# A gather-and-product kernel: from gathers tile by tile to gathers field by field over four tiles

## The chip, the cores and the metric

One core of a Trainium2 chip runs the kernel. The metric is the device time of one execution in microseconds (us); lower is better. Before the change the median of three runs is 652.37 us (652.29 to 653.44).

## The reference

A batch of 2048 samples, 26 index fields each, looks up 26 embedding rows of 32 float32 values; all pairs of rows of a sample are multiplied and summed; two weighted sums over rows and pairs go through a small network.

```python
embed = tables[jnp.arange(FIELD_NUM)[None, :], sparse_inputs]   # (2048, 26, 32)
p = jnp.einsum('bfe,bge->bfg', embed, embed)                    # (2048, 26, 26)
l_z = jnp.einsum('bfe,feh->bh', embed, w_z)                     # h = 256
l_p = jnp.einsum('bfg,fgh->bh', p, w_p)
l_1 = jax.nn.relu(jnp.concatenate([l_z + l_p + l_b, dense_inputs], axis=-1))
h = jax.nn.relu(l_1 @ W1 + b1)                                  # 128
return jax.nn.sigmoid(h @ Wf + bf)
```

Since p is symmetric, each pair is formed once and the two weights of a pair (`w_low`, `w_high`) are added on the chip.

## The kernel before

The samples are split in 16 tiles of 128 (one sample to a partition); four tiles make a round, because 4 x 128 columns fill one PSUM bank. All engines run their own program in order and meet at semaphores.

GpSimd (POOL, line 228) issues one indirect DMA for each tile and field, 416 in all, tile by tile and in a tile field by field. Each brings 128 rows of 32 values into `rows[:, t, 32 f : 32 (f+1)]`. The fields of a tile are two groups (0 to 15, and 16 to 25), each with one semaphore of `landed`. Before tiles 5 and 10 (`REST_BEFORE`) POOL waits until all that it has issued has landed.

ScalarE copies each landed group into PSUM (`copy_fields`, line 317). VectorE multiplies (`multiply`, line 259): for a chunk of fields g it forms the products with all fields up to the chunk's end, with one operand from the PSUM copy and the other from `rows`, and `add_up` (line 266) sums each product row of 32 into `pairs`. The chunks hold 4, 4, 4, 4, 3, 3, 2 and 2 fields, so a tile forms 383 pairs where 351 are different. The chunks make six stages; VectorE's order is multiply(stage s), then add_up(stage s-1).

TensorE turns the rows of a tile (`turn`, line 423, seven transposes by the identity into `ps_turn`), ScalarE moves them to `field_rows` (`lay_rows`, lines 174 and 175), and the same is done with `pairs` (`turn_pairs`, line 440, and `lay_pair_rows`, line 179). Once in a round TensorE sums over the fields (`sum_lz`, line 454, 14 matmuls) and over the pairs (`sum_lp`, line 465, 6 matmuls) into `ps_h0`; ScalarE applies the bias and relu (`make_hidden0`, line 340), TensorE makes `sum_h1` (lines 474 and 478), ScalarE `make_hidden1` (line 345), TensorE `sum_logit` (line 483), ScalarE the sigmoid (`make_scores`, line 351). SP stores all scores in one DMA.

ScalarE's order around these is written out by hand: the rows of tiles 4 to 7 are moved only at tiles 9 to 12, those of tiles 8 to 15 only after all 16 groups of copies. VectorE moves the second group of the last four tiles, and their pairs, after all its sums (`LATE`). So TensorE, in order, does the sums of rounds 2 and 3 after the last gather.

## Time and profile before

| what | us |
|---|---|
| median of three runs | 652.37 |
| the profiled execution | 652.55 |
| its span, first to last instruction | 650.8 |
| POOL busy in the span | 416.0 |
| VectorE busy | 436.1 |
| TensorE matmuls busy | 133.4 |
| ScalarE busy | 49.7 |

The profile is of one execution. "Busy" is the time in which an engine runs an instruction; "issue" in front of a gather is time that POOL spends between two gathers without waiting for anything that the profile shows. A line of a timeline has the start, the duration, the engine, the line of the kernel and the operation, and in brackets the idle time before it and what ended it. A float32 matmul has two records, so 14 matmuls stand as x28.

### The profile page before, as it was taken

What the parts mean: (1) busy time and instruction counts of PE and PEld (TensorE: products, weight loads), DVE (VectorE), ACT (ScalarE), POOL (GpSimd) and SP (SyncE); (2) the same over time, 40 slices, a digit from 0 to 9 for tenths busy, and PEclk for the clock granted to TensorE, in tenths of its full rate; (3) what the DMA queues carried; (4) which work ended last, traced back from release to release, by engine and by line L of the source; (5) the groups of instructions that cost most, each with busy time, mean ns of one, the idle gap of its engine ahead of it and who ended that gap; (6) DMA issues with size and microseconds to landing.
All of it is one profiled execution on the core that took longest, in us unless ns stands there. A gap on an engine that the chain in (4) does not pass through costs nothing.

```text
span 650.8 us, 1738 instructions
## 1 busy us (share of the span) xinstructions
PE 133.4 (21%) x356; PEld 62.2 (10%) x356; DVE 436.1 (67%) x249; ACT 49.7 (8%) x102; POOL 416.0 (64%) x423
## 2 busy tenths in 40 slices
PE   0000000063000000310302010100800000348996
PEld 0000000021000000100001010100300000124442
DVE  3378787878767878776958676776958767660010
ACT  0000101010000000001001020101000000013111
POOL 6777777777677777777776777777777777300000
PEclk9999999997555555565656555555955555578999
DMA  6212121212121212121111212111111111000000
GB/s 138 13 14 13 13 14 13 13 13 13 11 13 14 13 13 13 12 12 12 12 12 11 12 12 13 12 12 12 11 12 12 12 12 12 6 0 1 0 1 1
DMA packets 18200, 9.06 MB, mean 14 GB/s; under 512 B 9536, under 2 KB 18189, under 8 KB 18189
## 3 DMA queue, kind: packets, MB, share of 16 engines
q0 software_dynamic: 13312, 6.84, 15.6%
q1 hardware_dynamic: 4878, 2.11, 1.3%
q14 instruction: 7, 0.06, 0.0%
q8 instruction: 3, 0.05, 0.0%
HBM read 8.91 MB, written 0.01 MB: 14 GB/s over the span
## 4 chain that ended last, share of the span: by engine, by line
POOL 49%; issue 36%; PE 8%; another core or an unknown queue 3%; ACT 2%; DMA 1%; DVE 0%; ACTq 0%; POOLq 0%
POOL rows L228 49%; PE ps_h L454 4%; PE ps_h L465 2%; PE ps_turn L423 1%; PE ps_h L483 1%; PE ps_h L478 1%; ACT hidden L340 1%; ACT field_rows L175 1%; ACT ps_copy L317 1%; DMA rows<-in_L_rec_tables,which 1%; PE ps_pair L440 0%; PE ps_h L474 0%; DMA raw<-in_r_sparse_inputs 0%; ACT pair_rows L179 0%
## 5 line engine op out<-in xcount | busy, mean ns | idle before, releaser
L228 POOL DMA_INDIRECT rows<-in_L_rec_tables,which x416 | 415.2, 998 | 143.0 <-issue 137.8
L259 DVE TENSOR_TENSOR prod<-ps_copy,rows 128x1536 f32<-128x1536 f32 (+6 forms) x128 | 219.4, 1745 | 139.0 <-issue 110.8
L266 DVE TENSOR_REDUCE pairs<-prod 128x96 f32<-128x3072 f32 (+2 forms) x96 | 216.6, 2270 | 0.0
L423 PE MATMUL ps_turn<-ident,rows 128*128 128x128 f32 (+1 forms) x112 | 23.4, 360 | 221.2 <-DMA rows<-in_L_rec_tables,which 119.6
L465 PE MATMUL ps_h<-pair_rows,w_pair 128*128 128x512 f32 x48 | 25.4, 685 | 210.6 <-issue 209.4
L454 PE MATMUL ps_h<-field_rows,wz 128*128 128x512 f32 (+1 forms) x112 | 53.3, 632 | 35.6 <-issue 34.5
L317 ACT COPY ps_copy<-rows 128x512 f32<-128x512 f32 (+1 forms) x32 | 16.3, 509 | 528.8 <-DMA rows<-in_L_rec_tables,which 528.8
L423 PEld LDWEIGHTS ps_turn<-ident,rows 128*128 128x128 f32 (+1 forms) x112 | 16.6, 179 | 230.7 <-issue 209.6
L465 PEld LDWEIGHTS ps_h<-pair_rows,w_pair 128*128 128x128 f32 x48 | 10.3, 223 | 223.5 <-issue 221.8
L454 PEld LDWEIGHTS ps_h<-field_rows,wz 128*128 128x128 f32 (+1 forms) x112 | 22.0, 203 | 64.8 <-issue 64.8
L174 DVE COPY field_rows<-ps_turn 64x128 f32<-64x128 f32 x4 | 1.1, 283 | 37.7 <-PE ps_turn L423 37.7
L175 ACT COPY field_rows<-ps_turn 128x512 f32<-128x512 f32 (+1 forms) x28 | 13.7, 490 | 10.3 <-remote 9.2
L474 PE MATMUL ps_h<-dense_T,w_dense 13*128 13x512 f32 x8 | 5.6, 781 | 34.5 <-issue 30.3
L440 PE MATMUL ps_pair<-ident,pairs 128*128 128x128 f32 x48 | 11.2, 357 | 4.1 <-issue 4.1
L179 DVE COPY pair_rows<-ps_pair 128x384 f32<-128x384 f32 x4 | 2.2, 549 | 13.5 <-PE ps_pair L440 13.5
L478 PE MATMUL ps_h<-hidden,w 128*128 128x512 f32 x16 | 11.2, 839 | 0.0
L440 PEld LDWEIGHTS ps_pair<-ident,pairs 128*128 128x128 f32 x48 | 7.2, 182 | 12.4 <-issue 11.9
L340 ACT ACTIVATE hidden<-ps_h,lb_col 128x512 f32<-128x512 f32 x8 | 5.1, 683 | 34.4 <-PE ps_h L465 25.1
L179 ACT COPY pair_rows<-ps_pair 128x384 f32<-128x384 f32 x12 | 5.8, 484 | 13.1 <-PE ps_pair L440 12.8
L483 PE MATMUL ps_h<-hidden,wf 128*1 128x512 f32 x8 | 5.8, 813 | 0.8 <-ACT hidden L345 0.8
L278 DVE TENSOR_SCALAR dense_T<-ps_turn 13x512 f32<-13x512 f32 x4 | 2.7, 684 | 3.4 <-PE ps_turn L402 3.4
L474 PEld LDWEIGHTS ps_h<-dense_T,w_dense 13*128 13x128 f32 x8 | 1.4, 214 | 36.1 <-issue 30.5
(23 smaller groups left out, 24.9 us busy)
## 6 DMA issues: line engine op xcount, KB each, us to landing
rows<-in_L_rec_tables,which POOLq DMA_INDIRECT x416
wz<-in_L_rec_w_z SPq DMA_DIRECT2D x1, 768.0 KB
w_pair<-in_w_low SPq DMA_DIRECT2D x1, 384.0 KB
w_back<-in_w_high SPq DMA_DIRECT2D x1, 384.0 KB
raw<-in_r_sparse_inputs SPq DMA_DIRECT2D x1, 182.0 KB, 2.4
w<-in_L_rec_W SPq DMA_DIRECT2D x1, 128.0 KB
dense_in<-in_r_dense_inputs SPq DMA_DIRECT2D x1, 104.0 KB, 3.5
wz<-in_L_rec_w_z SPq DMA_DIRECT2D x1, 64.0 KB
```

The costliest lines, as they stand in the source:

```text
L175: return copy(field_rows[:, first:whole, k, :], ps_turn[:, g, 0:(whole - first) * P].rearrange("p (j b) -> p j b", b=P))
L228: nc.gpsimd.indirect_dma_start(rows[:, t, E * f:E * (f + 1)], None, table_rows, bass.IndirectOffsetOnAxis(ap=which[:, t, f:f + 1], axis=0) ...
L259: ins = nc.vector.tensor_tensor(made.rearrange("p (g f) e -> p g f e", f=f1), own.broadcast_to([P, f1 - f0, f1, E]), others.broadcast_to([ ...
L266: nc.vector.tensor_reduce(pairs[:, t, first:end], prod[:, (NS * t + s) % PRODS, 0:end - first, :], AX.X, ALU.add).then_inc(summed, 1)
L317: nc.scalar.copy(ps_copy[:, g, 0:E * (end - first)], rows[:, t, E * first:E * end])\
L340: ins = nc.scalar.activation(hidden0[:, h, :], ps_h0[:, h, :], ACT.Relu, bias=lb_col[:, h:h + 1])
L423: ins = nc.tensor.transpose(ps_turn[0:n, g, (j - first) * P:(j - first + 1) * P], rows[:, t, j * P:j * P + n], ident[:, :])
L440: ins = nc.tensor.transpose(ps_pair[:, c * P:(c + 1) * P], pairs[:, t, c * P:(c + 1) * P], ident[:, :])
L454: ins = nc.tensor.matmul(ps_h0[:, h, :], wz[0:n, j, h * P:(h + 1) * P], field_rows[0:n, j, :, :].rearrange("p t b -> p (t b)"), start=(j = ...
L465: ins = nc.tensor.matmul(ps_h0[:, h, :], w_pair[:, c, h * P:(h + 1) * P], pair_rows[:, c, :, :].rearrange("p t b -> p (t b)"), start=False ...
L478: ins = nc.tensor.matmul(ps_h1[:, :], w1[:, h, :], hidden0[:, h, :], start=False, stop=(h == HALVES - 1))
L483: nc.tensor.matmul(logit, wf[:, :], hidden1[:, :], start=True, stop=True).then_inc(logit_made, 1)
```

## The change

The order of the work becomes a round of four tiles, field by field. POOL gathers field f for the four tiles of the round, then field f+1. `rows` holds two rounds; from the third round on POOL waits until VectorE and TensorE have read the round before the last. Fields are grouped in units (four units of 4 fields, then 10 of one field), each with its own semaphore, and ScalarE copies a unit of all four tiles into one of four PSUM banks. `multiply` has one instruction for each field g over four tiles, with fields 0 to g, so that 351 pairs are formed; there are 18 stages a round, the last 12 of one field each. The waits for landed data before two of the tiles (`REST_BEFORE`) are gone.

The rows of fields 0 to 23 are turned by VectorE in blocks of 32 x 32 (`turn_rows`, 6 instructions a round, each over 128 partitions and 512 columns, into `rows_T`), and ScalarE puts the blocks in their places in `field_rows` (`lay_rows`, 32 copies a round of 32 partitions each: 16 of 512 columns and 16 of 256). The last two fields and the three blocks of pairs are turned by TensorE (4 transposes each) and evicted by ScalarE. TensorE's sums of a round are spread through it, and `sum_h1` begins with the dense part before it waits for `hidden0`.

```diff
-CHUNKS = [(0, 4), (4, 8), (8, 12), (12, 16), (16, 19), (19, 22), (22, 24), (24, 26)]
-STAGES = [(0, 3), (3, 4), (4, 5), (5, 6), (6, 7), (7, 8)]
+UNITS = [(0, 4), (4, 8), (8, 12), (12, 16)] + [(f, f + 1) for f in range(16, 26)]
+STAGES = [(0, 4), (4, 8), (8, 10), (10, 12), (12, 13), (13, 14)] + [(f, f + 1) for f in range(14, 26)]
...
-        rows = sb("rows", [P, TILES, NF * E])
+        rows = sb("rows", [P, 2, K, NF, E])
+        rows_T = sb("rows_T", [P, MOVED, K, PER, Q])
...
+            for r in range(ROUNDS):
...
+                if r >= 2:
+                    pool.wait_ge(multiplied, NS * (r - 1))
+                    pool.wait_ge(rows_turned, MOVED * (r - 1))
+                    pool.wait_ge(turned, TURNS * (r - 2) + ROW_TURN + 1)
                 for f in range(NF):
-                    nc.gpsimd.indirect_dma_start(
-                        rows[:, t, E * f:E * (f + 1)], None, table_rows,
-                        bass.IndirectOffsetOnAxis(ap=which[:, t, f:f + 1], axis=0),
-                    ).then_inc(landed[t][group_of(f)], DMA)
+                    for k in range(K):
+                        t = K * r + k
+                        nc.gpsimd.indirect_dma_start(
+                            rows[:, r % 2, k, f, :], None, table_rows,
+                            bass.IndirectOffsetOnAxis(ap=which[:, t, f:f + 1], axis=0),
+                        ).then_inc(landed[r][unit_of(f)], DMA)
...
+            def multiply(r, s):
+                n = NS * r + s
+                first, end = STAGES[s]
+                dve.wait_ge(copied, NU * r + unit_of(end - 1) + 1)
+                if n >= PRODS:
+                    dve.wait_ge(summed, n - PRODS + 1)
+                for g in range(first, end):
+                    u = unit_of(g)
+                    own = ps_copy[:, (NU * r + u) % COPIES, :, g - UNITS[u][0], :].rearrange("p k (o e) -> p k o e", o=1)
+                    at = pairs_before(g) - pairs_before(first)
+                    ins = nc.vector.tensor_tensor(products(n, s)[:, :, at:at + g + 1, :],
+                                                  own.broadcast_to([P, K, g + 1, E]),
+                                                  rows[:, r % 2, :, 0:g + 1, :], ALU.mult)
                 ins.then_inc(multiplied, 1)
...
+            def turn_rows(r, j):
+                n = chunk_fields(j)
+                for u in range(unit_of(PER * j), unit_of(PER * j + n - 1) + 1):
+                    first, end = UNITS[u]
+                    dve.wait_ge(landed[r][u], DMA * K * (end - first))
+                if r:
+                    dve.wait_ge(rows_laid, NM * (r - 1) + move_of(j) + 1)
+                nc.vector.transpose(rows_T[:, j, :, 0:n, :].rearrange("p k f b -> p k (f b)"),
+                                    rows[:, r % 2, :, PER * j:PER * j + n, :].rearrange("p k f e -> p k (f e)"))\
+                    .then_inc(rows_turned, 1)
...
+            for r in range(ROUNDS):
                 for s in range(NS + 1):
                     if s < NS:
+                        for j in range(MOVED):
+                            if s == stage_of(UNITS[unit_of(PER * j + chunk_fields(j) - 1)][0]):
+                                turn_rows(r, j)
+                        multiply(r, s)
                     if s:
+                        add_up(r, s - 1)
-            for t in range(LATE, TILES):
...
+            def lay_rows(r, m, q):
+                first, end = MOVES[m]
+                if q == 0:
+                    act.wait_ge(rows_turned, MOVED * r + end)
+                    if r:
+                        act.wait_ge(lz_summed, CH * (r - 1) + end)
+                for u in range(PER):
+                    n = sum(u < chunk_fields(j) for j in range(first, end))
+                    if n:
+                        ins = nc.scalar.copy(field_rows[Q * u:Q * (u + 1), first:first + n, :, Q * q:Q * (q + 1)],
+                                             rows_T[Q * q:Q * (q + 1), first:first + n, :, u, :])
...
+                for u, (first, end) in enumerate(UNITS):
+                    copy_fields(r, u)
+                    if r and first == 0:
+                        evict(r - 1, ROW_TURN)
+                        evict(r - 1, PAIR_TURN[-1])
+                    if r and first == 8:
+                        make_hidden0(r - 1)
+                    if 15 <= end - 1 < 19:
+                        lay_rows(r, 0, end - 16)
+                    if r and first == 17:
+                        make_hidden1(r - 1)
+                    if first == 19:
+                        evict(r, PAIR_TURN[0])
+                    if r and first == 20:
+                        make_scores(r - 1)
+                    if first == 23:
+                        lay_rows(r, 1, 0)
+                        lay_rows(r, 1, 1)
+                    if first == 24:
+                        lay_rows(r, 1, 2)
+                        lay_rows(r, 1, 3)
+                evict(r, PAIR_TURN[1])
...
+                turn_pairs(r, 0)
+                for j in range(*MOVES[0]):
+                    sum_lz(r, j)
+                sum_lp(r, 0)
+                turn_pairs(r, 1)
+                for j in range(*MOVES[1]):
+                    sum_lz(r, j)
+                turn_rows(r)
+                sum_lp(r, 1)
+                turn_pairs(r, BLOCKS - 1)
+                sum_lz(r, CH - 1)
+                sum_lp(r, BLOCKS - 1)
+                sum_h1(r)
+                sum_logit(r)
```

## Rows read from the trace of the kernel before

**Rows 1.** The page's chain of waits, shares of the span by engine.

```profile
POOL 49%; issue 36%; PE 8%; another core or an unknown queue 3%; ACT 2%; DMA 1%; DVE 0%; ACTq 0%; POOLq 0%
```

**Rows 2.** Busy us and count of instructions by engine, three stretches, PEclk after them.

```profile
3.60:258.10 254.50, 25.67 (x72) 13.63 (x72) 192.51 (x110) 13.32 (x30) 190.51 (x201) 0.80 0.22 20
258.10:560.00 301.90, 37.74 (x88) 17.21 (x88) 220.59 (x116) 17.55 (x37) 224.73 (x215) 0.55 0.17 12
560.00:651.00 91.00, 70.00 (x196) 31.35 (x196) 22.15 (x21) 17.54 (x34) 0.00 (x0) 0.88 0.00 1
```

**Rows 3.** Timeline: single gathers, and one VectorE operation beside the second.

```profile
3.64 1.10 POOL L228 DMA_INDIRECT rows<-in_L_rec_tables,which  x1 [2.05 <-DVE which L245]
...
14.89 0.96 DVE L283 TENSOR_TENSOR w_pair<-w_pair,w_back 128x768 f32<-128x768 f32 x1 [3.44 <-issue]
15.11 1.55 POOL L228 DMA_INDIRECT rows<-in_L_rec_tables,which  x1 [0.30 <-issue]
...
169.52 0.94 POOL L228 DMA_INDIRECT rows<-in_L_rec_tables,which  x1 [3.04 <-issue]
...
258.15 1.93 POOL L228 DMA_INDIRECT rows<-in_L_rec_tables,which  x1 [0.31 <-issue]
...
344.44 0.94 POOL L228 DMA_INDIRECT rows<-in_L_rec_tables,which  x1 [3.06 <-DMA rows<-in_L_rec_tables,which]
...
523.70 0.95 POOL L228 DMA_INDIRECT rows<-in_L_rec_tables,which  x1 [0.30 <-issue]
...
558.84 0.94 POOL L228 DMA_INDIRECT rows<-in_L_rec_tables,which  x1 [0.30 <-issue]
```

**Rows 4.** Groups by line and shape: busy us, mean ns of one.

```profile
L259 DVE TENSOR_TENSOR prod<-ps_copy,rows 128x512 f32<-128x512 f32 x16 | 11.1, 691 | 71.2 <-issue 71.2
L259 DVE TENSOR_TENSOR prod<-ps_copy,rows 128x2048 f32<-128x2048 f32 x16 | 36.5, 2279 | 0.0
L266 DVE TENSOR_REDUCE pairs<-prod 128x96 f32<-128x3072 f32 x16 | 53.5, 3341 | 0.0
L317 ACT COPY ps_copy<-rows 128x512 f32<-128x512 f32 x16 | 9.4, 589 | 324.8 <-DMA rows<-in_L_rec_tables,which 324.8
L317 ACT COPY ps_copy<-rows 128x320 f32<-128x320 f32 x16 | 6.9, 429 | 204.1 <-DMA rows<-in_L_rec_tables,which 204.1
```

**Rows 5.** Timeline of VectorE inside one tile.

```profile
108.56 2.35 DVE L259 TENSOR_TENSOR prod<-ps_copy,rows 128x2112 f32<-128x2112 f32 x1
110.83 2.04 DVE L266 TENSOR_REDUCE pairs<-prod 128x57 f32<-128x1824 f32 x1
```

**Rows 6.** Timeline after the last gather, all engines.

```profile
562.20 0.43 ACT L317 COPY ps_copy<-rows 128x320 f32<-128x320 f32 x1 [13.78 <-DMA rows<-in_L_rec_tables,which]
562.66 2.06 DVE L259 TENSOR_TENSOR prod<-ps_copy,rows 128x1824 f32<-128x1824 f32 x1 [5.27 <-ACT ps_copy L317]
563.09 7.68 PE L465 MATMUL ps_h<-pair_rows,w_pair 128*128 128x512 f32 x12 [93.74 <-issue]
...
576.77 3.53 DVE L266 TENSOR_REDUCE pairs<-prod 128x48 f32<-128x1536 f32 x2
...
583.50 1.12 PE L423 MATMUL ps_turn<-ident,rows 128*128 128x128 f32 x4 [5.13 <-ACT field_rows L175]
...
593.91 12.45 PE L454 MATMUL ps_h<-field_rows,wz 128*128 128x512 f32 x28 [0.55 <-ACT field_rows L175]
...
636.14 5.42 PE L465 MATMUL ps_h<-pair_rows,w_pair 128*128 128x512 f32 x12 [0.65 <-DVE pair_rows L179]
641.65 1.26 ACT L340 ACTIVATE hidden<-ps_h,lb_col 128x512 f32<-128x512 f32 x2 [19.54 <-PE ps_h L465]
...
646.04 0.69 ACT L345 ACTIVATE hidden<-ps_h,b_col 128x512 f32<-128x512 f32 x1 [3.13 <-PE ps_h L478]
646.78 1.02 PE L483 MATMUL ps_h<-hidden,wf 128*1 128x512 f32 x2 [0.78 <-ACT hidden L345]
647.84 1.10 ACT L351 ACTIVATE scores<-ps_h,bf_one 1x512 f32<-1x512 f32 x1 [1.11 <-PE ps_h L483]
```

More of the change, by code:

```diff
@@ new lines, in add_up @@
+            def add_up(r, s):
+                n = NS * r + s
+                first, end = (pairs_before(g) for g in STAGES[s])
+                dve.wait_ge(multiplied, n + 1)
+                if r and s == 0:
+                    dve.wait_ge(turned, TURNS * r)
+                nc.vector.tensor_reduce(pairs[:, :, first:end], products(n, s), AX.X, ALU.add).then_inc(summed, 1)
+            def turn_rows(r, j):
[8 more added lines that the diff above has]
+                    .then_inc(rows_turned, 1)
@@ L308, in _ @@
+                        multiply(r, s)
+                    if s:
+                        add_up(r, s - 1)
         @block.scalar
         def _(act):
-            def copy_fields(t):
-                for g in range(NG):
-                    first, end = group_fields(g)
-                    if t:
-                        act.wait_ge(multiplied, NS * (t - 1) + (FIRST_BANK if g == 0 else NS))
-                    act.wait_ge(landed[t][g], DMA * (end - first))
-                    nc.scalar.copy(ps_copy[:, g, 0:E * (end - first)], rows[:, t, E * first:E * end])\
-                        .then_inc(copied, 1)
@@ new lines, in sum_lz @@
+            def sum_lz(r, j):
+                if r == 0 and j == 0:
+                    pe.wait_ge(wz_in, DMA * 2)
+                if r and j == 0:
+                    pe.wait_ge(hidden0_made, HALVES * r)
+                if j < MOVED:
+                    pe.wait_ge(rows_laid, NM * r + move_of(j) + 1)
+                else:
+                    pe.wait_ge(evicted, TURNS * r + ROW_TURN + 1)
+                n = chunk_rows(j)
+                for h in range(HALVES):
+                    ins = nc.tensor.matmul(ps_h0[:, h, :], wz[0:n, j, h * P:(h + 1) * P],
+                                           field_rows[0:n, j, :, :].rearrange("p t b -> p (t b)"),
+                                           start=(j == 0), stop=False)
```

346 lines of the change are left out of this document (122 added, 224 removed).

## The prediction

> **What bounds the kernel now.** I read the chain of waits first. By engine, POOL's gathers hold 49% of it, "issue" 36% and TensorE 8% [rows 1]: the issue of gathers is the kernel for most of its length. Next, busy time by stretch [rows 2]. In the first two stretches, up to 560 us, POOL issues all its gathers (201 and 215) while VectorE is busy 192.5 of 254.5 and 220.6 of 301.9 us; in the third, 91 us, POOL does nothing, VectorE works 22 us and TensorE 70. So there are two parts, a part set by POOL and an end in which TensorE works off what ScalarE's and VectorE's orders put off. VectorE, though busy longer than POOL in total, waits on the gathers inside each tile.
>
> Single gathers give POOL's pace [rows 3]. The first starts at 3.64, the one after the first stretch at 258.15, the last at 558.84 us. The two waits for landed data show as idle 3.04 and 3.06 us instead of 0.30, so they cost 2.74 and 2.76 us. Without them the first 201 steps take 254.51 - 2.74 = 251.8 us, 1.25 us each; the next 214 take 300.69 - 2.76 = 297.9 us, 1.39 us each. From 258 us on, many gathers are stretched (the one at 258.15 is busy 1.93 us against 0.94). The trace doesn't name the cause, and it decides most of my range.
>
> The end [rows 6]: the last gather's data reach ScalarE at 562.20 (3.36 us after its start), VectorE's last sum ends at 576.77 + 3.53 = 580.3, and then two rounds' matmuls follow: 12.45 us for one `sum_lz`, 5.4 for one `sum_lp`, each twice, with transposes, copies and the network between. The span ends at 650.8, 92 us after the last gather began.
>
> **The change part by part.** The sum goes by the profiled execution, 652.55 us, which is 1.75 more than its span and 0.2 above the median.
>
> *Gathers.* Still 416, of the same form. The first index operations cover four tiles instead of two; by the 52- to 364-column cost they add a few tenths, so I start at 4.05. Both waits go: -5.5 us. What replaces them, the release of `rows` at rounds 2 and 3, asks for the round before the last, of which VectorE will be through some 20 us after its last gather, with 100 of the next round's 104 gathers still to go: nothing. With the stretched gathers as in the trace the last one starts at 4.05 + 251.8 + 297.9 = 553.8. If none is stretched it is 4.05 + 251.8 + 214 x 1.25 = 523.4; that is the lower bound. If all steps after the 201st are as stretched as the worst run of rows shows, see the rivals. I take the trace's value, since the instruction, its count and VectorE's load beside it stay nearly the same, and the trace shows no owner that the change removes.
>
> *VectorE.* A product instruction costs (2279 - 691) / 1536 = 1.034 ns a column, with 0.16 us on top [rows 4]; the reduce of 3072 columns fits the same line. The next starts 0.08 us before the former's end (2.27 us after one of 2.35 [rows 5]), so a step costs 1.034 ns a column + 0.08. A round has 351 pairs x 4 tiles x 32 = 44,928 columns to multiply and as many to add, 92.9 us, 44 instructions' 0.08, 3.5, and six transposes. The trace has no VectorE transpose. The nearest row is the 512-column product, 0.61 us net of overlap; I take 0.6, and as ends half (0.3) and twice (1.2) of it. Round: 100.0 us, against 109 now (436.1 / 4) and against 104 x 1.25 = 130 of gathers. VectorE stays the faster one, on average.
>
> The Trainium skill (VectorE: DVE Perf Modes, "The three transpose paths") gives 311 ns for one 128x128 bf16 block transpose; four of these would be 1.24 us by an estimate from that page, and adds 1.3 us to the end below. No row here shows it.
>
> But inside a round work grows with the field. After field g lands VectorE does the product of g and the sum of g-1, (2g + 1) x 0.1324 + 0.16 us: 5.3 at g = 19, 6.65 at 24, and 0.6 more at 19 and 23 for a transpose, against one field each 4 x 1.39 = 5.57 us. The backlog is 0.35 us when field 20 lands, 1.2 at 23, 3.7 at 25. After field 25: product 3.5, sum of 24 3.4, sum of 25 3.5. So VectorE ends 3.7 + 10.4 = 14.1 us after field 25 is in PSUM (17.5 us if the gathers step at 1.25, backlog 7.1). A round's surplus is absorbed by the next, whose first unit needs 16 gathers.
>
> *ScalarE.* Field 25's copy has 128 columns: 0.43 - 192 x 0.83 ns = 0.27 us (slope from the 512 and 320 column copies [rows 4]). It adds 32 partial copies a round, 16 x 0.59 + 16 x 0.375 = 15.4 us, and is idle nearly always; hidden. The risk is its order: eight copies (3.0 us) stand before the copy of field 24 and wait for the transpose of fields 20 to 23, which is behind VectorE's backlog. That puts field 24's copy about 1.2 + 0.6 + 3.0 + 0.3 = 5.1 us after field 23 was ready, while VectorE reaches it after 1.2 + 7.0: no wait.
>
> *TensorE.* 14 + 6 + 5 matmuls a round and few transposes, spread. In the last round `sum_lz` of fields 16 to 23 and the second block of pairs start when field 22's sum is done, about 15 us before VectorE's end, and need 1.1 + 4 x 1.8 + 1.1 + 2 x 1.8 = 13 us even at half clock (the granted clock of the second stretch is 0.55, that is mostly the 1.2 GHz level [rows 2]). They just fit.
>
> *After VectorE's last sum* [rows 6]: four transposes 1.12 and a hop 0.15; `sum_lz` of the last fields, 2 matmuls, under which the eviction (0.6) hides; `sum_lp` of the last block, 2 matmuls. A record is 12.45 / 28 = 0.44 us at full clock and 0.89 at half; the row at 563.09, first after an idle stretch, took 7.68 instead of 5.42, so five records at half. I take five of these eight at half: 5.8. Then relu 1.3, the last half of `sum_h1` 1.0, relu 0.74, logit 1.07, sigmoid 1.15 and the store to the span's end (650.8 - 648.94) 1.86. Sum 14.2 (11.4 all at full clock, 17.5 all at half).
>
> **Sum.** 553.8 + 3.36 + 0.30 (landing and copy) + 14.1 + 14.2 = 585.8 span, + 1.75 = 587.5 for a profiled execution, 587.3 as a median: **587 us**, 65 less than now. Of the 65, the end gives 60 (92 to 32), the waits 5.5.
>
> **The rivals.**
>
> *A. No stretched gathers.* What stretches them could be bound to tiles 7 and later, to their addresses in `rows` (up to 256 us none was stretched, with VectorE as busy), and `rows` shrinks to two rounds. Last gather 523.4, + 3.66 + 17.5 + 14.2 + 1.75 - 0.2 = 560 us. Against it: the trace may as well count time or gathers.
>
> *B. More stretching.* For: the gather at 15.11 was busy 1.55 us, 0.61 more than 0.94, beside a 0.96 us VectorE addition of two SBUF operands [rows 3]; transposes might do the same, 24 x 0.61 = 14.6: 602 us. And if all 415 steps take the 1.39 of the second stretch: 4.05 + 577 + 3.66 + 14.1 + 14.2 + 1.55 = 615 us. Against: products and sums run beside the first 201 gathers without a trace.
> The Trainium skill (SBUF — State Buffer, "SBUF: two separate sides") says that VectorE and GpSimd share a port pair as an exclusive lock, and that a VectorE operation in a two-port mode keeps GpSimd from writing DMA descriptors. By that rule the transposes, which read and write SBUF, would hold gathers up; it speaks for B, and the gather at 15.11 agrees with it; whether a transpose runs in such a mode no row shows.
>
> *C. VectorE becomes the bound, slower than before.* Place: `multiply`, whose instruction now spans four tiles, with a PSUM operand repeated over fields and stepped over tiles. Time is then 28 (first unit) + 4 x VectorE's round + 16, less where it is hidden. It reaches 652 when a round costs 152 us instead of 100, or 1.6 ns a column; at half rate, 2.07 ns, a round is 193 and the time some 816 us. Against: all product shapes of before, which already repeat and step, keep 1.03 ns. A transpose of 9 us would do it too.
>
> *D. The change doesn't shorten the end*, since TensorE's order leaves a round's sums behind VectorE's last. At half clock all 20 matmuls, 35 us, after it give 587 + 28 = 615, still faster. Against: the waits let 16 of them go before.
>
> **Chances.** Forecast (576 to 595) 0.45; A 0.25; B and D (595 to 640) 0.23; C 0.04; costs not seen here that cancel much or all of the gain, 0.03, a third of it on each side and a third at no change. Range: 557 to 613, from A with 3 us less in the end, to B's 615. Own range of the forecast 576 to 595, from the end's 11.4 to 17.5, the transposes' 0.3 to 1.2 and a third of the stretching more or less. A measurement of this kernel tells 0.2% (1.3 us) from nothing: faster 0.94, same 0.01, slower 0.05.
>
> **What would show it.** Right: POOL's last gather starts near 554, no idle of 3 us inside its queue, VectorE ends 18 us and the span 32 us after that gather. The gather steps in the profile after tell forecast (1.39 in the second half) from A (1.25 all through) and B (1.39 from the start). VectorE's transposes near 0.6 us, products on the line of 1.034 ns. Wrong: POOL idle at the start of rounds 2 or 3; VectorE idle under `copied` at fields 20 to 25; products over 1.1 ns a column; more than 18 us between VectorE's last sum and the end.

## The result and the profile after

The changed kernel took 694.21 us (median of 4 runs, 690.35 to 694.82) against 652.43 for the kernel before: ratio 1.0621, 95% interval 1.0598 to 1.0644, so 6% slower. The forecast was 587. The profiled execution took 694.79 us, its span 692.9.

What follows needs one fact ahead. Kernels of one series run on one chip beside the kernel before, and the kernel before took 652 to 654 us in six series, the first comparison among them, but 609.6 and 608.6 in two others. In those two the variants of the changed kernel are faster as well, and the changed kernel itself, measured in the second of them, wins: 573.63 against 608.6 us, 0.9439 (0.9402 to 0.9477). I call the first kind held and the second free, after what the traces show, and compare ratios only inside a series. The kernel before has no trace of the free kind.

The chain and three groups of the page, kernel after (the chain answers [rows 1]):

```profile
another core or an unknown queue 39%; issue 28%; POOL 13%; DVE 8%; ACT 7%; PE 2%; DMA 1%; DVEq 1%; ACTq 0%
...
L219 POOL DMA_INDIRECT rows<-in_L_rec_tables,which x416 | 426.0, 1024 | 132.3 <-issue 130.1
L254 DVE TENSOR_TENSOR prod<-ps_copy,rows 128x128 f32<-128x128 f32 (+12 forms) x104 | 199.4, 1943 | 197.7 <-issue 145.3
...
L276 DVE STREAM_TRANSPOSE rows_T<-rows 128x512 f32<-128x512 f32 x24 | 16.9, 702 | 59.3 <-issue 33.3
```

POOL's share of the chain fell from 49% to 13%, and the head is now a releaser that the profile can't name. VectorE is idle 197.7 us before its products, part of which it would wait for gathers in any case. The same stretches as [rows 2] (busy us and count for PE, PEld, DVE, ACT, POOL, then the granted clock):

```profile
3.70:258.00 254.30, 37.15 (x66) 15.28 (x66) 142.47 (x87) 34.66 (x70) 193.63 (x200) 0.76 0.26 20
258.00:560.00 302.00, 69.46 (x118) 26.78 (x118) 166.68 (x80) 41.65 (x89) 232.32 (x217) 0.57 0.19 12
560.00:693.00 133.00, 47.05 (x76) 16.96 (x76) 97.21 (x44) 29.03 (x58) 0.00 (x0) 0.58 0.00 0
```

POOL finishes as before, but VectorE has done 50 and 54 us less in the first two stretches and has 97 us left in the third, a whole round. The waits (engine, operation, releaser: us in total, times, longest) say whom VectorE and ScalarE waited for:

```profile
DVE prod L254 <- issue: 145.3, 6, 53.7
ACT pair_rows L349 <- remote: 131.7, 6, 33.4
...
ACT field_rows L343 <- remote: 63.6, 2, 32.5
```

L349 and L343 are ScalarE's evictions of what TensorE turned. "Remote" stands where no instruction in the trace ended when the wait did. Round 1's timeline shows why. TensorE's own records first (start, duration), then ScalarE's instructions that wait for them:

```profile
304.45 1.11 PE L424 MATMUL ps_turn<-ident,pairs 128*128 128x128 f32 x4 [27.47 <-issue]
306.97 5.55 PE L449 MATMUL ps_h<-field_rows,wz 128*128 128x512 f32 x8 [1.40 <-issue]
341.58 1.03 PE L434 MATMUL ps_turn<-ident,rows 128*64 128x128 f32 x4 [29.06 <-issue]
342.40 3.11 PE L459 MATMUL ps_h<-pair_rows,w_pair 128*128 128x512 f32 x4
375.20 1.08 PE L424 MATMUL ps_turn<-ident,pairs 128*128 128x128 f32 x4 [29.69 <-issue]
```

```profile
340.85 0.59 ACT L349 COPY pair_rows<-ps_turn 128x512 f32<-128x512 f32 x1 [33.35 <-remote]
...
374.48 0.58 ACT L343 COPY field_rows<-ps_turn 64x512 f32<-64x512 f32 x1 [32.55 <-issue]
396.88 0.59 ACT L349 COPY pair_rows<-ps_turn 128x512 f32<-128x512 f32 x1 [21.82 <-remote]
...
420.04 1.26 ACT L359 ACTIVATE hidden<-ps_h,lb_col 128x512 f32<-128x512 f32 x2 [21.57 <-remote]
...
437.48 0.69 ACT L366 ACTIVATE hidden<-ps_h,b_col 128x512 f32<-128x512 f32 x1 [7.79 <-remote]
...
520.08 0.59 ACT L349 COPY pair_rows<-ps_turn 128x512 f32<-128x512 f32 x1 [33.36 <-remote]
```

The turn of the pairs looks done at 304.45 + 1.11 = 305.6, yet ScalarE, which has had nothing else to do since 307.5, gets it at 340.85. Between that and the next eviction stand 12 records in TensorE's order (8 of `sum_lz`, 4 of `turn_rows`): 374.48 - 340.85 = 33.63 = 12 x 2.80. Then 8 records (`sum_lp` 4, `turn_pairs` 4): 22.40 = 8 x 2.80. From the eviction of one round's second block of pairs to that of the next round, 340.85 to 520.08, lie 179.23 us, and a round has 64 records: 2.80 again. So while the gathers run, TensorE's results come at 2.8 us a record, whatever the record's length, and the records' own times (1 to 6 us a group) hide it. Not from the start, though: the first turn of pairs, 109.16 to 110.25, is evicted at 110.29, and the next, done by its record at 150.51, only at 163.03, which is 28 records and 53.9 us after 109.16 instead of 78.4.

The lag ends some 27 us after the last gather began (558.86): the last waits for "remote" end at 574.68 and 586.67. VectorE around that time, and TensorE and ScalarE behind it:

```profile
521.19 1.68 DVE L254 TENSOR_TENSOR prod<-ps_copy,rows 128x128 f32<-128x128 f32 x4 [19.81 <-issue]
...
575.79 3.82 DVE L254 TENSOR_TENSOR prod<-ps_copy,rows 128x640 f32<-128x640 f32 x4 [52.30 <-ACT ps_copy L318]
...
615.63 1.11 PE L424 MATMUL ps_turn<-ident,pairs 128*128 128x128 f32 x4 [10.81 <-DVE pairs L266]
616.78 0.59 ACT L349 COPY pair_rows<-ps_turn 128x512 f32<-128x512 f32 x1 [7.49 <-PE ps_turn L424]
...
666.00 7.00 DVE L266 TENSOR_REDUCE pairs<-prod 128x100 f32<-128x3200 f32 x2
...
673.05 1.12 PE L424 MATMUL ps_turn<-ident,pairs 128*128 128x128 f32 x4 [9.43 <-DVE pairs L266]
...
689.99 1.11 ACT L372 ACTIVATE scores<-ps_h,bf_one 1x512 f32<-1x512 f32 x1 [1.96 <-PE ps_h L478]
```

Now 615.63 + 1.11 = 616.74 and the eviction starts at 616.78. But VectorE, whose last sum ended at 580.3 before [rows 6], has by 575.79 done only the products of the last round's first four fields (521.19); it stands still 52.3 us, since ScalarE's next copy (575.16) is behind evictions in its order, and ends at 673.0. The chain of the time is: evictions of the second block of pairs at 163.03, 340.85 and 520.08, that of the last round's first block at 616.78 (steps 177.8, 179.2, 96.7), then 76.1 us to the end.

### The profile page after: what moved, and what is told of

Same layout as the page of the kernel before. It is cut to its first block, busy times and chain, and to the rows that moved or that the text cites. A ratio compares the mean times of both kernels' runs of the same rounds, so it can differ in the third digit from the quotient of the medians.

```text
span 692.9 us, 1618 instructions
## 1 busy us (share of the span) xinstructions
PE 153.7 (22%) x260; PEld 59.0 (9%) x260; DVE 407.3 (59%) x213; ACT 106.6 (15%) x218; POOL 426.7 (62%) x423
## 3 DMA queue, kind: packets, MB, share of 16 engines
q0 software_dynamic: 13312, 6.84, 16.8%
## 4 chain that ended last, share of the span: by engine, by line
another core or an unknown queue 39%; issue 28%; POOL 13%; DVE 8%; ACT 7%; PE 2%; DMA 1%; DVEq 1%; ACTq 0%
POOL rows L219 13%; DVE pairs L266 5%; ACT field_rows L331 5%; DVE prod L254 3%; ACT ps_copy L318 2%; DMA rows<-in_L_rec_tables,which 1%; PE ps_h L473 1%; PE ps_h L459 1%; PE ps_h L449 1%; DVEq L90 1%; ACT scores L372 0%; PE ps_h L469 0%; PE ps_h L478 0%; DMA raw<-in_r_sparse_inputs 0%
## 5 line engine op out<-in xcount | busy, mean ns | idle before, releaser
L219 POOL DMA_INDIRECT rows<-in_L_rec_tables,which x416 | 426.0, 1024 | 132.3 <-issue 130.1
L254 DVE TENSOR_TENSOR prod<-ps_copy,rows 128x128 f32<-128x128 f32 (+12 forms) x104 | 199.4, 1943 | 197.7 <-issue 145.3
L266 DVE TENSOR_REDUCE pairs<-prod 128x76 f32<-128x2432 f32 (+7 forms) x72 | 196.9, 2739 | 0.0
L424 PE MATMUL ps_turn<-ident,pairs 128*128 128x128 f32 x48 | 13.3, 432 | 326.2 <-issue 244.3
L331 ACT COPY field_rows<-rows_T 32x512 f32<-32x512 f32 (+1 forms) x128 | 65.1, 509 | 88.6 <-issue 60.8
L449 PE MATMUL ps_h<-field_rows,wz 128*128 128x512 f32 (+1 forms) x112 | 74.2, 826 | 3.1 <-issue 2.1
L276 DVE STREAM_TRANSPOSE rows_T<-rows 128x512 f32<-128x512 f32 x24 | 16.9, 702 | 59.3 <-issue 33.3
L459 PE MATMUL ps_h<-pair_rows,w_pair 128*128 128x512 f32 x48 | 34.7, 864 | 53.8 <-issue 37.7
L318 ACT COPY ps_copy<-rows 128x128 f32<-128x128 f32 (+1 forms) x56 | 20.0, 365 | 123.5 <-DMA rows<-in_L_rec_tables,which 61.2
L424 PEld LDWEIGHTS ps_turn<-ident,pairs 128*128 128x128 f32 x48 | 8.6, 217 | 339.8 <-issue 250.1
L349 ACT COPY pair_rows<-ps_turn 128x512 f32<-128x512 f32 x12 | 7.0, 586 | 188.7 <-remote 131.7
L343 ACT COPY field_rows<-ps_turn 64x512 f32<-64x512 f32 x4 | 2.3, 579 | 100.5 <-remote 63.6
```

The lines of the kernel that those rows point to most:

```text
L219: nc.gpsimd.indirect_dma_start(rows[:, r % 2, k, f, :], None, table_rows, bass.IndirectOffsetOnAxis(ap=which[:, t, f:f + 1], axis=0),).the ...
L254: ins = nc.vector.tensor_tensor(products(n, s)[:, :, at:at + g + 1, :], own.broadcast_to([P, K, g + 1, E]), rows[:, r % 2, :, 0:g + 1, :], ...
L266: nc.vector.tensor_reduce(pairs[:, :, first:end], products(n, s), AX.X, ALU.add).then_inc(summed, 1)
L276: nc.vector.transpose(rows_T[:, j, :, 0:n, :].rearrange("p k f b -> p k (f b)"), rows[:, r % 2, :, PER * j:PER * j + n, :].rearrange("p k ...
L318: nc.scalar.copy(ps_copy[:, (NU * r + u) % COPIES, :, 0:end - first, :], rows[:, r % 2, :, first:end, :]).then_inc(copied, 1)
L331: ins = nc.scalar.copy(field_rows[Q * u:Q * (u + 1), first:first + n, :, Q * q:Q * (q + 1)], rows_T[Q * q:Q * (q + 1), first:first + n, :, ...
```

## Experiments

Held, first series (before 653.87). Theories: R, each TensorE record costs 2.8 us; I, each semaphore increment costs 11.2; L, the matmuls' own length.

**e1.** Half the increments (8 instead of 16 a round), with the waits counted anew:

```diff
-                ins.then_inc(lz_summed, 1)
+                if j == CH - 1:
+                    ins.then_inc(lz_summed, 1)
```

> The changed kernel with 8 TensorE semaphore increments a round instead of 16 (one for all of sum_lz, one for all of sum_lp; the matmuls are the same). In the trace after, TensorE's results reach ScalarE in steps of 11.2 us: 16 increments or, as well, 64 matmul records make the 180 us between two rounds. Theory R (2.8 us for each matmul record while gathers run): 64 records stay, so 180 us a round and 690 us, within 1%. Theory I (11.2 us for each increment): 8 x 11.2 = 90 us a round, under the 135 us of the gathers; the end shrinks to what was forecast and the time is 585 to 600 us.

695.27 us, ratio 1.0635 (1.0589 to 1.0681, from two runs), evictions at 340.91, 374.53 and 396.96 as in the changed kernel. I falls. (The Trainium skill, TensorE: Matmul & The Clock Gate, "The cost: per-tile semaphore tail", gives 26.3 ns for each increment where packed matmuls all raise a semaphore; eight fewer a round, 0.8 us a kernel by an estimate from that page, would not stand out here, and none did; the 2.8 us are a hundred times such a step.)

**e2.** 48 records, increments as they were. It leaves out the second half of the hidden columns in most field and pair sums:

```diff
-                for h in range(HALVES):
+                for h in range(HALVES if j == 0 else 1):
...
-                for h in range(HALVES):
+                for h in range(HALVES if c == BLOCKS - 1 else 1):
```

> The changed kernel with fewer matmuls and the same 16 increments a round: the second half of the hidden columns is left out of the sums but for the first chunk of sum_lz and the last block of sum_lp, so 48 matmul records a round instead of 64 (the output is not the reference's). Theory R: 48 x 2.8 = 134 us a round, about the gathers' own pace, time 590 to 620 us. Theory I: 16 x 11.2 = 179 us a round still, 690 us within 1%. If TensorE's late results come from its matmuls' own length (theory L), a quarter of it goes and the time is 640 to 670 us.

603.38 us, 0.9229 (0.919 to 0.9269): 16 records fewer a round and 91 us less. 48 x 2.8 = 134 us is below the 104 x 1.40 = 146 us that the stretched gathers take for a round. R holds; I and L, which gave 690 and 640 to 670, don't.

**e3, e4.** Plain DMAs of the same 16 KB in place of the indirect gathers, from SP's queue and from POOL's. Both fetch other rows than the reference's. The edit shown is e4's; e3 issues the same from SP, behind the same waits:

```diff
-                        nc.gpsimd.indirect_dma_start(
-                            rows[:, r % 2, k, f, :], None, table_rows,
-                            bass.IndirectOffsetOnAxis(ap=which[:, t, f:f + 1], axis=0),
-                        ).then_inc(landed[r][unit_of(f)], DMA)
+                        at = P * (NF * t + f)
+                        nc.gpsimd.dma_start(rows[:, r % 2, k, f, :], table_rows[at:at + P, :])\
+                            .then_inc(landed[r][unit_of(f)], DMA)
```

> The changed kernel with each of the 416 gathers replaced by a plain DMA of the same 16 KB issued by SP, from fixed table rows (the indices are not used, so the output is not the reference's). POOL is idle. If TensorE's results are late because gathers are generated on POOL (theories R and I), they come at once here: transposes are evicted within 1.5 us of their start, no 11.2 us steps, and the time goes by SP's issue or VectorE's 100 us a round: 400 to 450 us. If TensorE is late by itself (its matmuls, its clock, theory L), the steps of 11.2 us stay and the time is about 4 x 180 = 700 us.

> The changed kernel with each of the 416 gathers replaced by a plain DMA of the same 16 KB issued by POOL, from fixed table rows (the indices are not used, so the output is not the reference's). If it is POOL's software queue that holds TensorE's increments back, the steps of 11.2 us stay and the time is 600 to 700 us; if it is the indirect form alone, they go and the time is that of the run with SP's DMAs or of POOL's issue, 400 to 560 us.

446.49 us (0.683) and 441.84 (0.6758). VectorE is then the bound (406.3 of 437.9 us busy in e4). In e3 the same turn of pairs and its eviction, two rows of two views:

```profile
210.00 1.12 PE L424 MATMUL ps_turn<-ident,pairs 128*128 128x128 f32 x4 [28.87 <-DVE pairs L266]
```

```profile
211.15 0.59 ACT L349 COPY pair_rows<-ps_turn 128x512 f32<-128x512 f32 x1 [0.35 <-PE ps_turn L424]
```

64 records a round and no lag, so the matmuls' own length (L) is not it. In e4 POOL's queue moved the same 13312 packets and 6.84 MB as the gathers in the changed kernel, in steps of 0.53 us, and no wait of the trace ends with "remote". It takes indirect gathers to hold TensorE back; neither the matmuls nor POOL's queue and its packets as such do. (In both runs the kernel beside them was held.)

Held, second series (before 654.07).

**e5.** A fill of 1024 columns behind each gather, which the next gather waits for:

```diff
+                        n = K * (NF * r + f) + k
+                        if n:
+                            pool.wait_ge(spaced, n)
+                        nc.gpsimd.memset(spare[:, :], 0.0).then_inc(spaced, 1)
```

> The changed kernel with a memset of 128x1024 on POOL behind each gather, so that gathers come about half as often; the same 64 matmul records a round. The rounds become longer (416 times about 2.3 us, 900 to 1100 us in all), so the time decides nothing; what counts is the spacing of TensorE's results as ScalarE gets them. Theory R with a fixed cost: between a transpose of four records and the next result in a backlog still 11.2 us. Theory R with a cost that goes with the gathers' rate (each record waits for about 2.24 gathers): more than 11.2 if it counts gathers (about 20 us), less (about 5.6 us) if it is a share of something that gathers use up.

900.71 us (one run): 416 steps of 2.08 us are 865, and the tail. None of the three spacings expected came (11.2, 20 or 5.6 us): TensorE is prompt throughout and no gather is stretched (mean 952 ns against 1024), though POOL, with a fill behind each gather, runs an instruction every 1.04 us. The row and its eviction:

```profile
255.68 1.09 PE L430 MATMUL ps_turn<-ident,pairs 128*128 128x128 f32 x4 [30.35 <-ACT field_rows L349]
```

```profile
256.81 0.58 ACT L355 COPY pair_rows<-ps_turn 128x512 f32<-128x512 f32 x1 [1.27 <-PE ps_turn L430]
```

So on this one run the hold needs the gathers close behind one another.

**e6.** float32r operands for the field and pair sums, whose multiplications are then one record each instead of two: 44 records, nothing left out.

```diff
-        field_rows = sb("field_rows", [P, CH, K, P])
+        field_rows = sb("field_rows", [P, CH, K, P], mybir.dt.float32r)
-        pair_rows = sb("pair_rows", [P, BLOCKS, K, P])
+        pair_rows = sb("pair_rows", [P, BLOCKS, K, P], mybir.dt.float32r)
```

> The changed kernel with the operands of sum_lz and sum_lp rounded to float32r (written so by ScalarE's copies and by one conversion of the weights), so that each of these 20 matmuls is one record instead of two: 44 records a round. Theory R: 44 x 2.8 = 123 us a round, below the gathers' 130 to 145, TensorE no longer sets the round, 590 to 605 us. If float32r matmuls stay two records, or if another thing than records is counted, 690 us.

602.52 us, 0.9215 (0.9198 to 0.9231). Its last gather and VectorE's end:

```profile
560.84 0.94 POOL L221 DMA_INDIRECT rows<-in_L_rec_tables,which  x1 [0.30 <-issue]
```

```profile
579.75 7.00 DVE L268 TENSOR_REDUCE pairs<-prod 128x100 f32<-128x3200 f32 x2
```

**e7.** The pairs also turned by VectorE and laid by ScalarE, all float32: 52 records, but 48 more copies a round on ScalarE.

```diff
-                ins.then_inc(turned, 1)
...
+                nc.vector.transpose(pairs_T[:, c, :, :, :].rearrange("p k u b -> p k (u b)"),
+                                    pairs[:, :, P * c:P * (c + 1)]).then_inc(pairs_turned, 1)
```

> The changed kernel with the three blocks of pairs, too, turned by VectorE in 32x32 blocks and moved by ScalarE (48 more copies of 32 partitions x 128 columns a round, about 13 us), in full float32: 52 records a round. Theory R: 52 x 2.8 = 146 us a round, just above the gathers, 605 to 635 us. Otherwise (TensorE not the limit by records) 690 us or more, since ScalarE and VectorE get more work.

608.03 us, 0.9292 (0.9275 to 0.9308).

**e8.** The kernel before with float32r in its two sums (same edit as e6).

> The kernel before with the same float32r operands in sum_lz and sum_lp: 20 records less a round. Theory R: the kernel before too has TensorE's results late from its first sum_lz on; the records between 138 and 586 us fall from about 148 to 100, but ScalarE's order, written for late results, still puts two rounds' sums behind the last gather; these are half as long (2 x 9 us less): 625 to 638 us. If TensorE's lateness played no part before, the same 18 us less, so this run only bounds what the order costs.

627.58 us, 0.9585 (0.9558 to 0.9612): the kernel before also gains, though a third as much against its own time as the changed kernel does (694 to 602).

Free, third series (before 609.63).

**e9.** e6 and e7 together, 32 records.

> The two edits together: products of fields and pairs in float32r (a multiplication is one record) and the pairs turned by VectorE: 32 TensorE records a round instead of 64. Theory R (2.8 us a record while the gathers run): 32 x 2.8 = 90 us a round, far below the gathers' 130 to 145 us, so what is left is the gathers plus the tail. float32r alone (44 records, 123 us) gave 602.5 us, VectorE's turns alone 608.0: if TensorE was still late in either, this one is faster, 590 to 600 us; if both are bound by the gathers and by the last round's work on VectorE and ScalarE, nothing comes of it, 600 to 608 us. I take 602 us.

577.86 us, 0.948 (0.9461 to 0.9498), far below the 590 to 608 expected: the first sign that this series was of another kind.

**e10.** A quarter of the copies that lay the turned fields; three quarters of the laying is left out (a fill of `field_rows` with 0.5 stands at the start instead).

```diff
-                for u in range(PER):
+                for u in range(1):
```

> The changed kernel with a quarter of ScalarE's copies that lay the turned fields (8 instead of 32 a round; it leaves three quarters of the laying out and TensorE multiplies what stands there). TensorE's 64 records a round stay. Theory P (each engine is held for itself, 2.8 us per TensorE record whatever the others do): TensorE's results still come 11.2 us apart per four records, 690 to 697 us. Theory S (the engines share one limit while the gathers run, so that fewer instructions on ScalarE leave more to TensorE and POOL): TensorE's steps fall below 10 us and the time to 640 to 680 us. I take P, 693 us.

579.26 us, 0.9493 (0.9458 to 0.9529). By the time alone this looks like S. It isn't: all kernels of the series were fast, the kernel before too, and with TensorE prompt in all three traces nothing could tell P from S.

**e11.** e5 with a fill of 128 columns.

> The changed kernel with a short fill of 128 columns on POOL behind every gather (0.1 to 0.2 us and a wait of the next gather's slot), so that a gather starts every 1.4 to 1.6 us instead of every 1.25 to 1.40. With the long fill (2.08 us a step, 900 us) TensorE's results were prompt: 255.68 + 1.09 = 256.77, evicted at 256.81. Theory T (TensorE is held only while the gathers are issued back to back, any pause frees it): prompt again, and the time is 416 x 1.5 + 33 = 657 us (616 to 700), below the changed kernel's 694 although each gather costs more. Theory U (it takes the long pause): 2.8 us a record as before, 695 to 720 us. I take T.

606.68 us, 0.9965 (0.9943 to 0.9986), below the 616 to 700 of T, and prompt, but in this series so was everything. T isn't shown.

The fourth series was held (before 652.71).

**e12.** The changed kernel, no edit.

> The changed kernel itself once more, beside a kernel before. In one series of runs the kernel before took 609.6 us instead of 652 to 654, its gathers never left 1.25 us and TensorE's results came 0.1 us after its records. Theory C (the hold on TensorE belongs to the chip that a series runs on, or to its condition, and comes and goes with the kernel before's 653 or 610 us): where the kernel before takes about 610 us the changed one takes 576 to 585 us (the gathers' last start at 539 plus the 40 us that the float32r version showed from there); where the kernel before takes about 653, the changed one takes 694 again. Theory D (the three edited kernels of that series were fast by their edits): 640 us or more beside a before of 610.

690.35 us, 1.0575 (1.0541 to 1.0609).

**e13.** e10 once more.

> The kernel with 8 instead of 32 laying copies a round once more (it leaves three quarters of the laying out). If the kernel before takes about 653 us here, then P (each engine held for itself): 690 to 697 us with TensorE's results 11.2 us apart per four records; S (one limit that the engines share): 640 to 680 us. If the kernel before takes about 610 us: 579 us as before, and P and S aren't told apart.

694.74 us, 1.0634 (1.06 to 1.0669), 115 us more than the very same kernel took in the free series. The evictions:

```profile
344.65 0.59 ACT L352 COPY pair_rows<-ps_turn 128x512 f32<-128x512 f32 x1 [40.47 <-remote]
...
378.28 0.58 ACT L346 COPY field_rows<-ps_turn 64x512 f32<-64x512 f32 x1 [32.55 <-issue]
...
400.68 0.59 ACT L352 COPY pair_rows<-ps_turn 128x512 f32<-128x512 f32 x1 [21.82 <-remote]
```

33.63 us for 12 records and 22.40 for 8, to the hundredth as with four times the laying copies. P holds: fewer copies on ScalarE give nothing back to TensorE.

The fifth was free (before 608.60).

**e14, e15.** e9 and e11 again.

> float32r products and pairs turned by VectorE (32 TensorE records a round), where the kernel before takes about 653 us: 32 x 2.8 = 90 us a round is far below the gathers' 130 to 145 us. If TensorE was what the single edits (602.5 and 608.0 us there) had left late, 590 to 600 us; if the gathers' end at 561 us and the last round's work set it, 600 to 608 us. I take 601 us. Where the kernel before takes about 610 us: 578 us again.

> The changed kernel with the short fill behind every gather (a gather every 1.33 us at the least), where the kernel before takes about 653 us. Theory T (any pause between gathers frees TensorE): its results come within 0.2 us of its records and the time is 600 to 640 us. Theory U (only a long pause as that of the 2.08 us step does): 2.8 us a record as in the changed kernel, 690 to 720 us. I take U by the other series, in which the hold was absent with and without the pause and nothing speaks for T. Where the kernel before takes about 610 us: 607 us again.

577.29 us (0.9487) and 606.21 (0.9969), as in the third series. The 577.29 is more than the 573.63 of the changed kernel in the same series (e16), so where nothing is held the two edits gain nothing. Whether the short pause lifts the hold stays open.

**e16.** The changed kernel again, no edit.

> The changed kernel beside the kernel before of this series. Theory C (the hold goes with the chip or its condition): 576 to 585 us where the kernel before takes about 610, 690 to 695 where it takes about 653.

573.63 us, 0.9439 (0.9402 to 0.9477). C holds, 2.4 us below its range: the same kernel is 6% slower than the kernel before in held series and 6% faster in a free one. Which series is which does not go by the chip alone: by the record the first two series, held, and the fifth, free, ran on the chip of the same number. Its trace, TensorE's records of round 1 and ScalarE's evictions:

```profile
279.17 1.12 PE L424 MATMUL ps_turn<-ident,pairs 128*128 128x128 f32 x4 [29.05 <-DVE pairs L266]
280.08 5.53 PE L449 MATMUL ps_h<-field_rows,wz 128*128 128x512 f32 x8
285.44 0.60 PE L434 MATMUL ps_turn<-ident,rows 128*64 128x128 f32 x4
```

```profile
280.33 0.59 ACT L349 COPY pair_rows<-ps_turn 128x512 f32<-128x512 f32 x1 [0.34 <-PE ps_turn L424]
286.08 0.58 ACT L343 COPY field_rows<-ps_turn 64x512 f32<-64x512 f32 x1 [0.15 <-PE ps_turn L434]
```

The two evictions that lay 33.63 us apart are 5.75 apart. POOL's last gather and VectorE in the last round:

```profile
522.54 0.94 POOL L219 DMA_INDIRECT rows<-in_L_rec_tables,which  x1 [0.30 <-issue]
```

```profile
476.19 0.71 DVE L276 STREAM_TRANSPOSE rows_T<-rows 128x512 f32<-128x512 f32 x1 [7.01 <-DMA rows<-in_L_rec_tables,which]
476.87 1.89 DVE L254 TENSOR_TENSOR prod<-ps_copy,rows 128x1664 f32<-128x1664 f32 x1
...
545.27 3.62 DVE L254 TENSOR_TENSOR prod<-ps_copy,rows 128x3328 f32<-128x3328 f32 x1
548.80 7.00 DVE L266 TENSOR_REDUCE pairs<-prod 128x100 f32<-128x3200 f32 x2
```

The gathers keep the 1.25 us (mean 946 ns), so the stretching belongs to the held kind too.

**e17.** e9 where it is held (before 652.60).

> float32r products and pairs turned by VectorE (32 TensorE records a round) where the kernel before takes about 653 us: 590 to 600 us if TensorE had been late in the single edits (602.5 and 608.0 us), 600 to 608 if the gathers' end at 561 us and the last round's work set it; I take 601. Where the kernel before takes about 610: 577 us.

609.75 us, 0.9347 (0.9326 to 0.9369), against 601 expected. Fewer records did not help beyond e6. Of the 6.5 us of span more than in e6, 3.5 lie behind VectorE's last sum (17.5 us against 14.0), where the last block is turned by VectorE and laid by sixteen copies; 3.0 come before it, for VectorE's last sum ends at 589.75 instead of 586.75. What delays it there is not shown; one suspect is ScalarE. Three of its sixteen copies of a block of pairs in e17, and all of them in e9:

```profile
440.54 0.30 ACT L367 CAST pair_rows<-pairs_T 32x128 fp32r<-32x128 f32 x1 [1.10 <-issue]
441.95 0.30 ACT L367 CAST pair_rows<-pairs_T 32x128 fp32r<-32x128 f32 x1 [1.12 <-issue]
443.35 0.30 ACT L367 CAST pair_rows<-pairs_T 32x128 fp32r<-32x128 f32 x1 [1.09 <-issue]
```

```profile
151.00 4.91 ACT L367 CAST pair_rows<-pairs_T 32x128 fp32r<-32x128 f32 x16
```

0.31 us a copy in the free series, 1.40 in the held one. ScalarE is held as well: its idle under "issue" before these copies is 167.6 us in e17, and in e9 no such entry stands among its waits. But it is held only after some fifteen instructions in a row. In the changed kernel's own trace fourteen laying copies of 0.41 us and a field's copy between them run back to back, and then the steps become 1.0 and 1.40:

```profile
143.00 3.31 ACT L331 COPY field_rows<-rows_T 32x256 f32<-32x256 f32 x8 [15.36 <-issue]
...
146.61 2.47 ACT L331 COPY field_rows<-rows_T 32x256 f32<-32x256 f32 x6
149.69 0.40 ACT L331 COPY field_rows<-rows_T 32x256 f32<-32x256 f32 x1 [0.60 <-issue]
151.09 0.40 ACT L331 COPY field_rows<-rows_T 32x256 f32<-32x256 f32 x1 [1.00 <-issue]
```

**e18.** e6 once more, held (before 653.39).

> The changed kernel with float32r products (44 TensorE records a round), the best version where the kernel before takes 653 us (602.5 there, ratio 0.9215). Where the kernel before takes about 610 us: the changed kernel took 573.6 and its gathers' last start was at about 537 with 33 us from there, of which TensorE's last products in float32 are a few us: 568 to 574 us, ratio 0.93 to 0.945. Where it takes about 653: 602.5 again.

602.01 us, 0.9214 (0.919 to 0.9237). It is the best version that computes all of the reference where held; in a free series it was not measured.

## Why the prediction was wrong

*TensorE: the step that failed.* "They just fit", and for ScalarE's order "no wait", priced TensorE's groups at their records' busy time. In the held runs a round of 64 records costs 64 x 2.80 = 179 us, above the gathers' 130 to 145. ScalarE's order puts evictions and hidden layers between the copies for which VectorE waits, so VectorE stood still (19.8 and 52.3 us before the first two units of the last round alone) and did nearly all of the last round after the gathers. The forecast gave slower a chance of 0.05 and named no such cause. Rival D had the place, TensorE's order, but the wrong price, half-clock matmuls: the granted clock is 0.57 in the second stretch after and 0.55 before, and isn't what changed. Rival C was slower by VectorE's rate, and VectorE's rate was as forecast.

The kernel before had the same hold. There a result that looks ready comes late as well; of its timeline, TensorE's turn and the eviction of it:

```profile
570.60 0.93 PE L423 MATMUL ps_turn<-ident,rows 128*128 128x128 f32 x7
```

```profile
582.86 0.58 ACT L175 COPY field_rows<-ps_turn 128x512 f32<-128x512 f32 x1 [9.23 <-remote]
```

It lost less, 44 us between the kinds where the changed kernel lost 120. In both some 30 to 36 us of that are the stretched gathers (558.86 against 522.54 for the last one, after and e16), so the late results cost the changed kernel about 84 and the kernel before some 14; these are estimates (30 is 558.84 less rival A's 523.4 and the waits' 5.5), as the kernel before has no free trace. A likely reason, not tested, is that it puts two rounds' sums behind the last gather, where TensorE is prompt [rows 6], and keeps records off the gathers' time: 88 records stand in its second stretch [rows 2], 118 in that of after. I read its 92 us at the end as waste that the change would recover; 60 of the 65 us forecast came from there. The 3% "another core or an unknown queue" [rows 1], on one core, was the sign I passed over.

*With the hold out of the way the terms can be read one by one.* e6 has the records few enough (it is another program: four records fewer behind VectorE's last sum), e16 is the changed kernel itself:

| term | forecast | e6, held | rival A | e16, free |
|---|---|---|---|---|
| last gather starts | 553.8 | 560.84 | 523.4 | 522.54 |
| from there to VectorE's end | 17.8 | 25.9 | 21.2 | 33.3 |
| from there to the span's end | 14.2 | 14.0 | 14.2 | 16.1 |
| span | 585.8 | 600.7 | 558.8 | 571.9 |

- *Gathers*: the two waits are gone (no idle of POOL above 0.9 us inside its queue, 3.0 before [rows 3]), but the 5.5 us taken off for them were not gained: the last gather starts at 558.86, before at 558.84, and in the nine other held traces of both kernels and their variants with back-to-back gathers at 558.64 to 561.26. The forecast let the first 201 steps take 1.25 us and the rest 1.39. The traces bear another reading: POOL may run ahead of a pace of 1.40 us by some 18 gathers and then keeps to that pace. After, the first stretched gather is the 175th, at 222.14, and (222.14 - 3.74) / 1.40 = 156, so it is 18 ahead; the 241 steps from there to the last take 1.40 each. Before, the gather at 258.15 has 201 ahead of it where 1.40 gives 182, so 19; a wait of 2.7 us on the way only put the stretching off. Rival A's 1.25 us throughout is exact in the free series. Its reason, tile or address, is not: the same program has the stretching in held runs and not in free ones. For the release of `rows`, 20 us are 16 gathers, so 88 and not 100 were still to go; nothing waited there.
- *Transposes beside gathers* (B): they don't hold them up. In e16, 32 gathers run beside the 24 transposes, none busy above 0.95 us. The addition at the start does: the gather beside it is busy 1.60 us in the changed kernel and 1.32 in e16, and ends 0.8 us after the addition in both, as in [rows 3].
- *VectorE's costs* were right. The 3328-column product took 3.61 us, and 1.034 ns x 3328 + 0.16 is 3.60 [rows 4]. A transpose took 0.70 us against 0.6. (The Trainium skill, VectorE: DVE Perf Modes, "The three transpose paths", gives 311 ns for 128x128 in bf16, 1.24 us for this size by an estimate from it; the 0.70 measured in float32 decides.)
- *VectorE's backlog* was too small by 8 us in e6 and 12 in e16. I let it begin at field 19. But fields 12 to 15 form one unit, and in e16 their data come together at 476.19, with four products and four sums (and the former stage's) still to do; field 16's product starts at 493.77, only when they are through, while a field's gathers take 5.0 us. The gap never closes: field 25's product starts at 545.27, 19.1 us after its data (522.54 + 3.66).
- *The end* was within its bounds of 11.4 to 17.5 in e6 (with half the records that the forecast counted) and e16. In the changed kernel itself it is 19.9 us (673.0 to 692.9): the eight records behind the turn all run at the lower clock (7.5 us instead of 5.8), and both halves of the last `sum_h1` stand behind the hidden layer at that clock, 3.8 us instead of the 1.0 I took.

So in a free series the forecast's 587 would have been 13 us too high with the right sign, and that partly by luck: its gathers 31 us too late, VectorE's end and the last stretch 17 us too short. In the held kind the sign was wrong.

## What to carry to other kernels

Where indirect gathers run back to back, read when TensorE's result reaches its reader and not when its record ends; divide the gap between two readers by the records between them. Waits put down to "remote" or "unknown queue" in a program on one core are such a place. Before work is moved from behind the gathers to beside them, count its instructions on each engine, and compare with the gathers' time for a round; fewer instructions (float32r's one record for two) pay there, for the length of one made no difference. Rerun a comparison beside its base on another occasion before its sign is believed: here 1.062 and 0.944 are the same two programs.

## What the runs showed of the hardware

- In held series, with indirect gathers every 1.25 to 1.40 us, TensorE's results came at 2.80 us a record (33.63 for 12, 22.40 for 8, 179.23 for 64), until some 27 us after the last gather. A record has a weight load and a matmul, two instructions. ScalarE's copies of 0.30 us stepped at 1.40, and gathers came to 1.40 a step (mean 1024 ns busy instead of 946).
- None was held at once: POOL was some 18 gathers ahead of the 1.40 us pace before its first stretched one, ScalarE ran fifteen copies back to back before its first late one, and TensorE's first late result came 24.5 us, 17 instructions of 1.40, earlier than 2.80 us a record from 109.16 on would give. One instruction of an engine per 1.40 us, each engine for itself, with room to run ten to twenty ahead, would give all of this; that is a reading of the numbers and not shown. What inside the chip does it is open. One rival no run tests: every run on record was read by the profiler (each has a span and a granted clock), so whether the hold is there when nothing is recorded is not known.
- It was absent with plain DMAs from SP and from POOL (e3, e4), with gathers 2.08 us apart (e5), and in two whole series (e9 to e11, e14 to e16), the unedited changed kernel among them. What makes a series held or free is open; it moved the kernel before by 44 us and the changed one by 120.
